# A graph network's second half: edge ends loaded in eleven parts, and a nearer wait ahead of the gathers

## What is computed

```
out    = concat([x2[src], edge_attr], axis=1)
out    = selu(out @ W1a + b1a) @ W1b + b1b
summed = segment_sum(out, dst)
mean   = summed / maximum(counts, 1)
h      = concat([x2, mean, u[batch]], axis=1)
x      = layernorm(x2 + selu(h @ W2a + b2a) @ W2b + b2b)
```

## Time and profile before

| | |
|---|---|
| median of 3 runs | 2644.59 us (2637.71 to 2650.03) |
| profiled execution | 2639.33 us, span 2637.6 us |
| PE busy | 2112.2 us (80%) |
| POOL busy | 1821.8 us (69%) |
| DVE busy | 1552.7 us (59%) |
| ACT busy | 986.8 us (37%) |
| data moved | 346.45 MB, 131 GB/s in the mean |

### The profile page before, as it was taken

The page is one execution under the profiler, slowest core; times in us unless marked ns, Lnnn a source line. Parts: engine busy times, 40 slices in busy tenths (PEclk is TensorE's granted clock), DMA queues, the critical chain, the costliest instruction groups (busy, mean ns, idle before and its releaser), DMA issues. The chain is left out here.

```text
span 2637.6 us, 52060 instructions
## 1 busy us (share of the span) xinstructions
PE 2112.2 (80%) x18382; PEld 1552.2 (59%) x18382; DVE 1552.7 (59%) x3098; ACT 986.8 (37%) x2255; POOL 1821.8 (69%) x1853
## 2 busy tenths in 40 slices
PE   1899999999969999946787877887877778766753
PEld 1555555555535555535676666666666666656753
DVE  6889999984435554554555555555555555543433
ACT  3777787780000000032333333333333333322322
POOL 5437766646655676777777777777777777777775
PEclk9999999999989999957988889889888988886665
DMA  8375787788696776434333333333333333332212
GB/s 291 125 228 201 207 252 238 208 235 225 220 188 208 231 231 228 141 94 117 74 71 69 70 64 79 66 68 77 68 68 74 72 67 74 66 67 51 52 42 45
DMA packets 478172, 346.45 MB, mean 131 GB/s; under 512 B 357844, under 2 KB 428687, under 8 KB 474253
## 3 DMA queue, kind: packets, MB, share of 16 engines
q1 hardware_dynamic: 367443, 272.49, 36.4%
q0 software_dynamic: 54240, 57.23, 10.0%
q10 hardware_dynamic: 56250, 13.52, 2.5%
HBM read 200.58 MB, written 142.39 MB: 130 GB/s over the span
## 5 line engine op out<-in xcount | busy, mean ns | idle before, releaser
L982 POOL DMA_INDIRECT A_sb<-source_terms,src_cur x1172 | 1119.9, 956 | 357.3 <-issue 350.9
L932 POOL DMA_INDIRECT sorted_edges<-pm_row,pm_to x440 | 482.5, 1097 | 199.3 <-issue 83.9
L1863 DVE TENSOR_TENSOR arena<-iota_code,arena 128x2048 f16<-128x2048 f16 (+1 forms) x392 | 438.1, 1186 | 27.7 <-PE cnt_ps L1410 25.3
L1077 ACT ACTIVATE A_sb<-cnt_ps 128x392 f32 (+1 forms) x784 | 383.7, 498 | 124.5 <-PE cnt_ps L1410 74.5
L1539 PE MATMUL agg_ps<-A_sb,arena 128*128 128x448 f16 x1911 | 379.3, 356 | 23.9 <-DMA A_sb<-counts_matrix 23.9
L2180 DVE TENSOR_TENSOR cnt_ps<-cnt_ps,A_sb 128x512 f32<-128x512 f32 x147 | 102.1, 694 | 444.8 <-DMA A_sb<-source_terms,src_cur 439.8
L1639 PE MATMUL agg_ps<-A_sb 128*65 128x48 f32 x2344 | 196.8, 245 | 180.4 <-DVE A_sb L2193 180.4
L1223 ACT ACTIVATE A_sb<-cnt_ps 128x512 f32<-128x512 f32 x147 | 87.4, 595 | 643.4 <-DVE cnt_ps L2180 643.2
L1410 PEld LDWEIGHTS cnt_ps<-arena 128*128 128x128 f16 x3136 | 190.0, 100 | 213.4 <-issue 164.3
L1410 PE MATMUL cnt_ps<-arena 128*128 128x98 f16 x3136 | 280.2, 214 | 32.9 <-ACT A_sb L1077 25.7
L1639 PEld LDWEIGHTS agg_ps<-A_sb 128*65 128x65 f32 x2344 | 182.7, 161 | 202.3 <-DVE A_sb L2193 197.2
(11 more groups left out here) (308 smaller groups left out, 3302.4 us busy)
## 6 DMA issues: line engine op xcount, KB each, us to landing
counts_matrix<-A_sb SPq DMA_DIRECT2D x14, 5488.0 KB, 17.3
A_sb<-counts_matrix SPq DMA_DIRECT2D x12, 5488.0 KB, 19.4
arena<-in_edge_attr_dram SPq DMA_DIRECT2D x96, 256.0 KB, 2.8
sorted_edges<-zrow SPq DMA_DIRECT2D x11, 1716.0 KB
A_sb<-source_terms,src_cur POOLq DMA_INDIRECT x1172
arena<-sorted_edges SPq DMA_DIRECT2D x143, 128.0 KB
overlapping_rows<-A_sb SPq DMA_DIRECT2D x1, 13056.0 KB, 39.4
A_sb<-in_edge_attr_dram SPq DMA_DIRECT2D x50, 256.0 KB, 2.8
```

The costliest lines, as they stand in the source:

```text
L932: pool.indirect_dma_start(out=sorted_d, out_offset=bass.IndirectOffsetOnAxis(ap=pm_to[:, k, j:j + 1], axis=0), in_=pm_row[:, k, j, :], in_ ...
L982: pool.indirect_dma_start(out=gath[k][:, j * F:(j + 1) * F], out_offset=None, in_=p_d, in_offset=bass.IndirectOffsetOnAxis(ap=src_cur[k][: ...
L1077: act.activation(Asb(half)[:, :, bass.ds((b * BG + k) * GROUP, GROUP)].rearrange("p b (w j) -> p b w j", j=PAIR), cnt_ps[k % 2][:, 0:SUB * ...
L1863: ins = dve.tensor_tensor(hot_rows[:, slots], iota_code[:, 0:n, :].unsqueeze(1).to_broadcast([P, AT_ONCE * SUB // 2, n, 2]), turned[:, bas ...
```

## The change

The loads of the 201 full groups of ends are split into eleven parts of 18 or 19 groups for the sources and the same for the destinations. One part of each is issued in every block from 3 to 13, right behind that block's counts matrix. The short last group and the bases stay where they were. The semaphore `edges_in` now ends at 416 instead of 96. In the edge stage the wait ahead of the gathers of group g asks for one more finished group: it now waits for the sums of group g - 2.

```diff
+END_PARTS = NSB - 3
+ENDS_IN = 16 * 2 * (END_PARTS + 2)
...
                 if s < NSB - 1:
                     sp.dma_start(A_sb[:, 1 - half, :], A_d[bass.ds(s - 1, 1), :, :].rearrange("a p n -> (a p) n")).then_inc(A_in[1 - half], 16)
+                if s >= NSB - END_PARTS:
+                    load_ends(s - (NSB - END_PARTS))
                 sp.wait_ge(x2_ready, s + 1)
...
+            def load_ends(part):
+                first, end = gE * part // END_PARTS, gE * (part + 1) // END_PARTS
+                for to, frm in ((src_e, src), (dst_e, dst)):
+                    sp.dma_start(to[:, first:end, :], frm[first * EG:end * EG].rearrange("(g p j) -> p g j", p=P, j=EJ)).then_inc(edges_in, 16)
+
             for to, frm in ((src_e, src), (dst_e, dst)):
-                sp.dma_start(to[:, 0:gE, :], frm[0:gE * EG].rearrange("(g p j) -> p g j", p=P, j=EJ)).then_inc(edges_in, 16)
                 sp.dma_start(to[0:TROWS_IN, gE, 0:TJ], frm[gE * EG:E - TREST].rearrange("(p j) -> p j", j=TJ)).then_inc(edges_in, 16)
...
-            pool.wait_ge(edges_in, 96)
+            pool.wait_ge(edges_in, ENDS_IN)
...
-                pool.wait_ge(seg_ready, g - 2)
+                pool.wait_ge(seg_ready, g - 1)
```

More of the change, by code:

```diff
@@ L519, in general_begins @@
             eng.wait_ge(pq_ready, NSB)
-            eng.wait_ge(edges_in, 96)
+            eng.wait_ge(edges_in, ENDS_IN)
         def general_ends(eng):
@@ L1270, in fin_root @@
                 act.activation(st4[:, 2, cols, :], st4[:, 1, cols, :], ACT.Sqrt, bias=eps_t[0:CH, 0:1], scale=1.0 / F).then_inc(std4, 1)
-            act.wait_ge(edges_in, 96)
+            act.wait_ge(edges_in, ENDS_IN)
             for h in range(DEEP):
@@ L2136, in _ @@
             dve.wait_ge(base_in, 32)
-            dve.wait_ge(edges_in, 96)
+            dve.wait_ge(edges_in, ENDS_IN)
             step(dve.memset(ones_r, 1.0))
```

## The result

The changed kernel takes 2712.65 us (median of 4 runs, 2708.59 to 2715.96), the kernel before 2642.27 in the same session. The ratio is 1.0263, with a 95% interval from 1.0240 to 1.0286: 2.6% slower. The prediction was 2695 with a range from 2661 to 2733. The profiled execution took 2710.38 us, with a span of 2708.6.

A forecast was written before the change was run, and what follows sets the result against it. PE was taken to bound the kernel up to about 1140 us, then POOL's gather issue. 2639.3 - 26 + 80 = 2693, put at 2695 us for a median, own range 2670 to 2720, wider range 2661 to 2733.

The forecast's parts named there:

- The two regimes: Whole kernel: PE sets the pace up to about 1140 us, afterwards perhaps POOL.
- the queue of SP as the hole's cause: Layer 2: PE waits 23.94 us for the counts matrix because SP issues two loads of all edge ends first.
- POOL's own issue as the pace of the edge stage: Edge stage: 1172 gathers at 1.26 us each; POOL's issue, not the transfers, sets the pace.
- the pause once per heavy slot: Edge stage: POOL pauses once per four slots, at those with two unit steps, 28 times 2.86 us.
- Edit 1: Layer 2, ends in eleven parts: PE's wait for the counts matrix and a restart at lower clock go, -26 us.
- edit 2: Edge stage, POOL's wait one group nearer: gathers overlap late sums in 28 slots, +80 us, bounds 28 to 125.
- Nothing is late next: PE itself is: Layer 2: once PE's wait for the counts matrix goes, no other engine holds PE up.
- The parts' issue: SP's queue, layer 2: each load of a part takes about 2 us to issue at most; cost 0, bounds 0 to +5.
- every heavy slot becomes a slot 104: Edge stage rival: PE's idle gaps bring low clock in every slot with two unit steps; +125, 2738 us, chance 0.13.
- the high-clock rival: Edge stage: high clock and short lag everywhere, +28 us, so the two edits cancel at 2641 us; chance 0.08.
- the backlog rival: Edge stage: the sums' lag was carried-over work that the first pause clears, wait then free; 2613 us, chance 0.03.
- the one in which edit 1 does nothing: Layer 2: the counts matrix might still be late, held by the base load or the parts; 2719 us, chance 0.05.

The follow-up runs named there:

- Edit 1 alone: Ends loaded in eleven parts, POOL's wait left at three groups back, against the kernel before: 2630.66 us, ratio 0.9952.
- a kernel that wins 4.1% there: Whole change plus PE summing the group before the second unit step in two-step slots, against the kernel before: 0.9586 (3191.89 us) there, 1.0123 on the first chip.

## Why the prediction was right, and where it was not

**Sign and cause held, the size by luck in part.** The two regimes, the queue of SP as the hole's cause, POOL's own issue as the pace of the edge stage, and the pause once per heavy slot are all in the trace after. Edit 1 alone is faster, and edit 2, by the difference, costs several times that. The total was off by only 18 us because the terms that were too small (the restart, 23 us, the early pauses, 2, and the 5 us lost of edit 1) met one that was too large by 14.

**Edit 1: -26 expected, -21 in layer 2, -14 timed alone.** The matrix was issued near 734 and its wait went, as said. The failed step is "Nothing is late next: PE itself is". POOL was late next, with some 33 us of scatters a block against PE's 33.0, and its lateness reached PE by ACT's load and copy. I had looked for what else SP delays, not for who had caught up during the hole. Two blocks from 730.61 to 803.09 take 72.5 us instead of 66.0; that gives back 6.5 of the 26.1. Putting the load behind the copy brought the whole term (27.5 us between the stores, 25.6 timed).

**The parts' issue: 2 us expected, 17 to 19 measured, cost 0 as expected.** I had divided the 15 to 18 us of the earlier trace rows by eleven, as if the hold went with the size of the load itself. Each second part waits where the 5.5 MB of the matrix went ahead, as the small loads did behind the ends before; in block 13, without a matrix, it took 1.38. What stands behind it is needed a block later, so nothing came of it.

**Edit 2: +80 expected, +92 in the stage, +82 by the timed runs.** The mechanism was right, the size came from two errors of opposite sign. The bare overlap was smaller: 88.7 us of pauses behind the 28 heavy slots, less 28 x 0.82 of restart, is 65.7, or 2.35 each instead of 2.86. I had taken the mean of the 20 slots of before that began on time; four of those had the short lag, of the 28 after the change nine had it, and no overlap was over 3.5 us where six had been over 3.9. And the restart, 0.82 us after the sums' end, was missing: 28 x 0.82 = 23 us. My price was the bare overlap, as if POOL started in the moment the sums end. The two early pauses, of which I had dropped one, give 2.

**The clock.** The granted clock decides the pause: in slots 96, 100 and 104 it was 1.00, 0.71 and 0.62 up to the end of the sums, and the pauses were 1.7, 3.5 and 4.1 us. The rule of the Trainium skill ("TensorE: Matmul & The Clock Gate", section "Why this matters for your kernels"), that idle gaps bring the clock down, held for 11 of 28 slots, with some 5 us of idle ahead of the unit sums, and in part for 8, with 3.1 to 3.6. The other 9 had only 1.0 to 1.7 us of idle there, so they are no test of it. What failed was my step from the rule to "every heavy slot becomes a slot 104": the idle time ahead of the unit sums was not the same from one heavy slot to the next. The rival that it led to, +125 and 2738 us, is not what happened. Nor did the high-clock rival (2641), the backlog rival (2613) or the one in which edit 1 does nothing (2719; its time is nearer to 2712.65 than my 2695 is, but the first gather 20.7 us earlier and edit 1 alone at 0.9952 speak against it).

**The sum.** -21 + 92 = +71 on the profiled execution, where I had -26 + 80 = +54.

## What to carry to other kernels

A hole on the critical path is also the time in which others catch up: before it is counted as gained, look for the engine whose work per round is as long as the bound's, and for the wait by which it would reach it. A wait moved one group nearer costs its overlap each time, and the price is read by laying the end of one event beside the start of the other; add the restart, which is due even where the two only touch. And a wait ahead of a load, placed before a copy that another engine needs, is a debt that shows only when all else is on time.

## What the runs showed that I had not expected

- POOL's gather that waits starts 0.82 us after the end of the awaited sums: in every one of the 30 pauses, where the sums were 0.07 us late (0.89 lost), and where they ended 0.41 us before POOL was ready (0.41 lost). A wait is free, beside the usual 0.30, only when it was met 0.82 us ahead.
- SP's queue takes the matrix (5488 KB) and one more load of 18 x 8 numbers a partition at once, and holds the next for 17 to 19 us. Without the matrix ahead the next took 1.38.
- The same program takes 2642 us on one chip and 3328 to 3380 on another, with PE idle where the profile shows nothing awaited. Edit 2, +3.1% on the first by the difference of two ratios, is within 0.3% of the kernel before on the other, and a kernel that wins 4.1% there costs 1.2% on the first.
- The first store of the terms, which closes a part that no run changed, lay between 697 and 708 us in the profiles on ordinary chips. That alone puts up to 11 us between two profiles. Its cause stays open.
